# Attention with a written-out engine order: the scores of a pair's first unit are issued after the projection, the output projection and the values

## The reference

```
q = rope(x @ wq)      # 32 heads of 128
k = rope(x @ wk)      # 8 heads of 128, each shared by 4 query heads
v = x @ wv
scores = q k^T * 128**-0.5, masked to (j <= i) & (j > i - 128)
out = softmax(scores) @ v @ wo
x = layernorm(x + out)
```

## Time and profile before

| what | value |
|---|---|
| time, median of 3 runs | 2449.51 us (2446.68 to 2454.55) |
| profiled execution: span, first to last instruction | 2436.7 us |
| first attention in it, from the first scores to the last oproj | about 55.9 to 866 us |
| PE's granted clock, mean over the span | 0.824 |
| PE busy, share of the span | 71% |

### The profile page before, as it was taken

The page is one execution under the profiler, slowest core; times in us unless marked ns, Lnnn a source line. Parts: engine busy times, 40 slices in busy tenths (PEclk is TensorE's granted clock), DMA queues, the critical chain, the costliest instruction groups (busy, mean ns, idle before and its releaser), DMA issues. The chain is left out here.

```text
span 2436.7 us, 25968 instructions
## 1 busy us (share of the span) xinstructions
PE 1735.8 (71%) x7274; PEld 1296.7 (53%) x7274; DVE 1618.9 (66%) x3711; ACT 1291.9 (53%) x3343; POOL 1019.0 (42%) x699
## 2 busy tenths in 40 slices
PE   5888888888888869997685455425644633566997
PEld 4777777777777658886552222212322311334885
DVE  3677766776666645556435888898788879742335
ACT  3556555465554433333337777876677788433221
POOL 3435445354443435553203343346433334632442
PEclk9999999999999979998855667657766756788998
DMA  3112111111110112221400000010000000001111
GB/s 148 31 42 69 53 56 47 41 55 65 56 46 17 57 61 95 103 77 53 113 20 7 7 7 1 12 16 7 7 7 7 7 1 7 1 1 44 39 52 47
DMA packets 33570, 96.40 MB, mean 40 GB/s; under 512 B 4048, under 2 KB 16720, under 8 KB 29264
## 3 DMA queue, kind: packets, MB, share of 16 engines
q1 hardware_dynamic: 33456, 95.20, 11.8%
HBM read 87.84 MB, written 7.34 MB: 39 GB/s over the span
## 5 line engine op out<-in xcount | busy, mean ns | idle before, releaser
L198 PE MATMUL PS<-AR 128*128 128x512 f32 (+2 forms) x2568 | 559.5, 373 | 172.6 <-issue 71.6
L198 PE MATMUL PS<-XT,AR 128*128 128x512 f32 x2472 | 633.6, 412 | 24.1 <-POOL AR L796 12.3
L198 PEld LDWEIGHTS PS<-AR 128*128 128x128 f32 x2568 | 454.0, 199 | 270.3 <-issue 158.2
L198 PEld LDWEIGHTS PS<-XT,AR 128*128 128x128 f32 x2472 | 482.1, 198 | 140.0 <-issue 14.4
L1235 POOL TENSOR_TENSOR AF<-AF 128x512 f32<-128x512 f32 (+3 forms) x64 | 148.4, 2319 | 487.5 <-DVE AF L1440 487.5
L1043 PE MATMUL PS<-AR,XT 48*128 48x128 f32 (+3 forms) x256 | 129.0, 504 | 139.6 <-DVE BF L1303 72.5
L1176 ACT ACTIVATE AF<-PS 128x512 f32<-128x512 f32 x160 | 94.0, 594 | 252.4 <-PE PS L1056 130.5
L546 POOL TENSOR_TENSOR AF<-AF 128x512 f32<-128x512 f32 x80 | 103.2, 1291 | 255.8 <-ACT AF L338 255.8
L1071 PE MATMUL PS<-AF,BF 128*128 128x512 f32 x320 | 189.7, 697 | 20.8 <-ACT AF L1176 20.8
L1091 PE MATMUL PS<-BF,AF 128*128 128x1 f32 x24 | 7.0, 362 | 265.2 <-DVE BF L1401 265.2
L552 POOL TENSOR_TENSOR AF<-AF 128x512 f32<-128x512 f32 (+1 forms) x64 | 107.5, 1680 | 178.2 <-DVE AF L681 178.2
(11 more groups left out here) (171 smaller groups left out, 3635.0 us busy)
## 6 DMA issues: line engine op xcount, KB each, us to landing
AF<-in_mean_w SPq DMA_DIRECT2D x48, 448.0 KB, 3.3
AF<-in_ffn_w SPq DMA_DIRECT2D x14, 1536.0 KB, 6.3
AF<-in_attn_w SPq DMA_DIRECT2D x9, 1536.0 KB, 6.7
AF<-in_attn_w SPq DMA_DIRECT2D x9, 1024.0 KB, 5.2
AF<-in_ffn_w SPq DMA_DIRECT2D x11, 769.0 KB, 4.4
XT<-rope_scratch SPq DMA_DIRECT2D x96, 64.0 KB, 2.8
rope_scratch<-BF SPq DMA_DIRECT2D x20, 256.0 KB, 2.3
AF<-in_x SPq DMA_DIRECT2D x8, 256.0 KB, 4.1
```

The source lines that it names most:

```text
L198: last = nc.tensor.matmul(dst, lhs(a, c), rhs(m, c), start=(first and k == 0), stop=(k == 3 * n - 1 and not more))
```

## The change

In every unit with i = 0 but the very first (n = 0), PE issues its scores after turn_p(n-1), the projection of the query head, oproj(n-2) and pv(n-1), and before the key's projection. The wait for `R0["lo"]` moves with them. On DVE, pt_lo(n-1) is put ahead of the wait for the scores in these units; it came right behind the mask. That is 15 of the 64 units. Nothing is added or removed.

```diff
--- before.py
+++ after.py
@@ -386,14 +386,19 @@
                     n = NU * g + u
                     bb = 2 * g + b
 
-                    pe.wait_ge(R0["lo"], 5 * bb + 5)
-                    wait(pe, A0["masked"], n)
-                    lo = 1 if i == 0 else 0
-                    for h in range(G0):
-                        dst = PS[:, h // 2, (h % 2) * 256 + lo * P:(h % 2) * 256 + 256]
-                        last = mm3(dst, lambda a, c: qT[:, b, a, h, i * P:(i + 1) * P],
-                                   lambda m, c: kT[:, b, m, (i - 1 + lo) * P:(i + 1) * P], 1)
-                    last.then_inc(A0["scores"], 1)
+                    def scores():
+                        pe.wait_ge(R0["lo"], 5 * bb + 5)
+                        wait(pe, A0["masked"], n)
+                        lo = 1 if i == 0 else 0
+                        for h in range(G0):
+                            dst = PS[:, h // 2, (h % 2) * 256 + lo * P:(h % 2) * 256 + 256]
+                            last = mm3(dst, lambda a, c: qT[:, b, a, h, i * P:(i + 1) * P],
+                                       lambda m, c: kT[:, b, m, (i - 1 + lo) * P:(i + 1) * P], 1)
+                        last.then_inc(A0["scores"], 1)
+
+                    late = i == 0 and not (first and u == 0)
+                    if not late:
+                        scores()
                     if not (first and u == 0):
                         turn_p(n - 1, (u - 1) % QT)
                     nb, j = (b + 1) % 2, i
@@ -405,6 +410,8 @@
                         oproj(n - 2, g if u > 1 else g - 1)
                     if not (first and u == 0):
                         pv(n - 1, (u - 1) % QT, ((u - 1) // QT) % 2)
+                    if late:
+                        scores()
                     if has_next:
                         if j == 0:
                             pe_proj_item(pe, ng, bb + 1, nb, "k", 0, 5 * (bb + 1) + 1)
@@ -657,13 +664,16 @@
                     if last_group and u >= 3:
                         norm_stats(dve, 1, u - 3, u - 3, A0["yadd"], n - 2)
                     k0 = 1 if i == 0 else 0
+                    late = i == 0 and not (first and u == 0)
+                    if late:
+                        pt_lo(n - 1, (u - 1) % QT)
 
                     dve.wait_ge(A0["scores"], n + 1)
                     src = PS[:, 0:2, :].rearrange("p a (h k) -> p (a h) k", h=2)[:, :, k0 * P:256]
                     nc.vector.tensor_tensor(Sm[:, u % 2, :, k0 * P:256], src,
                                             mask0[:, k0 * P:256].unsqueeze(1).to_broadcast([P, G0, (2 - k0) * P]),
                                             ALU.add).then_inc(A0["masked"], 1)
-                    if not (first and u == 0):
+                    if not (first and u == 0) and not late:
                         pt_lo(n - 1, (u - 1) % QT)
                     dve.wait_ge(A0["masked"], n + 1)
                     wait(dve, A0["exp"], n)
```

## The result

The changed kernel takes 2452.49 us (median of 18 runs, 2449.75 to 2463.36), the kernel before beside it 2445.95 us (18 runs): ratio 1.0027, 95% interval 1.0014 to 1.0040. It is slower, by 6.6 us (6.5 between the medians), within what I had called no change. The forecast was 2470 us, 21 us slower. The profiled execution has a span of 2454.9 us, 18.2 us over that of the kernel before, but in the first attention, from the first mask to the end of the stage (its last oproj runs from 868.3 to 871.2 us in the kernel before, later than the 866 in the table ahead of the prediction), the two differ by only 819.7 - 814.5 = 5.2 us. The other 13 us lie in stages with the same instructions; they differ as single executions do, since the medians don't show them.

What follows compares the result with a forecast made beforehand. PE was taken as the limit in stretches, alternating with a late chain through DVE, ACT and POOL. 14 x 1.33 + 2.4 = 21.0 us, clock terms cancelling, on 2449.5 gave 2470 us; range 2446 to 2490.

Steps and rivals of the forecast that it cites:

- Step 1: At PE's start of a pair, the wait for L616 becomes one for pnorm, 2.86 us not 3.49: gain 0.63 us.
- Steps 2 and 3: Late scores delay ACT's exponentials and the key's swap queued behind them: oproj(n-1) 1.33 us later in each pair.
- Step 4: Last group's second pair, without projections: later scores and their chain put turn_p(60) at 834.4, not 832.15: +2.4 us.
- Step 5: PE's clock: the shorter wait at pair starts saves 6.9 us, new waits ahead of oproj cost 7.0; the two cancel.
- steps 1 to 4: The sum at the same clock over the stage: 14 x 1.33 + 2.4 = 21.0 us slower.
- partly back: Rival on PE's clock: a third to a half of its loss returns, the shift stays: 2453 to 2459 us, chance 0.12.
- the first rival: The clock falls at each new wait ahead of oproj as well, at the dearer price: 43 us, 2493 us, chance 0.18.

Runs made afterwards that it cites:

- e2_after_fill: Changed kernel with 10 extra matmuls, not part of the computation, ahead of turn_p in the 15 units: 2441.88 us, ratio 0.9969 to the kernel before.
- e1_before_fill: Kernel before with 12 extra matmuls put into PE's wait ahead of the late scores in the 15 units: 2418.39 us, ratio 0.9867.
- e3_scores_mid: Changed kernel with the late scores right behind the projection, ahead of oproj and pv: 2427.39 us, ratio 0.9914 to the kernel before.
- e5: e2_after_fill with four small copies on ScalarE ahead of the exponentials of the 15 late units: 2452.09 us, ratio 1.0011 to the kernel before.
- e9: e3_scores_mid with four small copies on ScalarE ahead of the exponentials of the 15 late units: 2430.71 us, ratio 0.9913 to the kernel before.
- e4_proj_first: e3_scores_mid with the query projection moved ahead of turn_p in the late units: 2377.84 us, ratio 0.9709 to the kernel before.
- e8_proj_first_fill: e4_proj_first with six extra matmuls in the wait for the output weights' low part, once in seven groups: 2366.17 us, ratio 0.9654 to the kernel before.

## Why the prediction was off

- **Step 1** (gain 0.63 us, the wait is now for pnorm): right, 2.87 us in place of 2.86.
- **Steps 2 and 3** (the chain behind the late scores holds the key's swap, +1.33 us a pair): right. 2.57 us a group in place of 2.66 at full clock; e2_after_fill against e1_before_fill has the whole of it in the runs, e3_scores_mid takes it back, and e5 and e9 show that the chain is on the path in the changed order and off it with the scores ahead of oproj.
- **Step 4** (the last pair, +2.4 us; its own terms add up to 2.3): from PE's last instruction of the pair before to turn_p(60) it is 837.83 - (824.86 - 2.87) = 15.84 us, and was 832.15 - (822.33 - 4.09) = 13.91: +1.9 us.
- **Step 5** (the clock: -6.9 and +7.0, "the two cancel"): wrong, and this is the term that was mis-sized. From a late pair's start to its turn_p(n) the kernel before takes 13.49 us at full clock, and in the 14 pairs with projections 34.4 us more than that in sum. The changed kernel takes 14.49 us, as at 259.79 and 310.87, and in the 14 pairs 16.4 us more. I took a fifth of the loss to come back; it was 18.0 of 34.4, half. Of the new waits ahead of oproj one of seven lost the clock, and one wait for the weights: 3.0 us, not 7.0. In sum -15.0 in place of +0.1. The two waits, in the timeline of PE:

```profile
791.40 5.01 PE L198 MATMUL PS<-AR 128*128 128x512 f32 x15 [2.55 <-DVE AF L633]
...
806.35 5.98 PE L198 MATMUL PS<-AR 128*128 128x512 f32 x18 [2.03 <-POOL AR L315]
```

With the 21.0 us forecast for steps 1 to 4 that makes 6.0 us, and with what these steps measured, 7 x 2.57 + 1.9 = 19.9, it makes 4.9. The stage took 5.2 us longer in the profiled execution, and the runs say 6.6. It is the case put down as "partly back", a third to a half of the loss (here 15.0 of 34.4), to which I had given 0.12. PE's busy time over the loop points the same way: 12.3 us less on the same matmuls, at a mean granted clock of 0.97 in place of 0.95 (windows of the kernel before, then of the changed one):

```profile
154.69:822.33 667.64, 584.91 (x2874) 488.68 (x2874) 461.54 (x575) 357.44 (x862) 307.56 (x238) 0.95 0.14 48
```

```profile
155.39:824.83 669.44, 572.62 (x2873) 473.81 (x2873) 453.56 (x575) 357.67 (x862) 307.60 (x238) 0.97 0.14 48
```

The error in the argument was to read a threshold of idle time off two rows. That 2.86 us lie nearer to 3.08 than to 1.97 said little: the clock fell behind 2.87 us at ten pairs and held at four. The rows of the kernel before gave a sign of it: behind the same 3.5 us the 12 matmuls of the scores took 2.81 us at one pair's start and 1.55 at the next one's, where the clock fell only later. Nor was the first rival, a fall at each new wait, an idle one: in e2_after_fill that same wait lost the clock in six of seven groups.

By "TensorE: Matmul & The Clock Gate" of the Trainium skill, section "Why this matters for your kernels", a gap of 2.87 us keeps the clock; the trace agrees at four starts and not at ten, and the falls behind 2.0 us are against it.

## What to carry to other kernels

When a wait is moved on the engine that limits, ask what stands next in its list and when that is ready: here it was ready 0.6 us before, so that 3.5 us of waiting hid 2.9. And ask what hangs on the step that is made late, through the in-order queues of the engines behind it: the scores fed a chain that stood ahead of the key's swap. The step to put into such a wait is one that needs nothing of the work before, and feeds nothing that is late; the query projection was one, and was worth some ten times what the change cost.

## What the runs showed of the hardware

Between 2.0 and 2.9 us, the length of a wait does not tell whether TensorE's clock falls behind it. Behind the 2.0 us for the output weights it held in all seven groups of the kernel before and fell in six of seven of e1_before_fill and all seven of e4_proj_first, with the same instructions around it. Behind 2.87 us it fell in ten of fourteen pairs of the changed kernel and in seven of fourteen of e3_scores_mid. Behind the 3.5 us of the kernel before it fell in all fourteen, and behind waits of 1.74 us and less in none of the fourteen pairs, whichever the kernel. A fall cost 1.3 to 3.2 us each time. Filling a wait with matmuls that nobody reads kept the clock up behind that wait, and was worth 31 us in e1_before_fill and 13 in e8_proj_first_fill. What places the fall was not tested.
